# First phase of a fused MetaFormer kernel: projection and residual one slot later, values last in slot 1, tie break and block scaling in fewer instructions

## The reference

```
value, feat = conv1x1(x, v_w, v_b), conv1x1(x, f_w, f_b)      # heads of 24 channels, image in 2 x 2 quarters
centers, value_centers = pool(feat), pool(value)               # 2 x 2 centres of each quarter
sim = sigmoid(beta + alpha * einsum('bmc,bnc->bmn', l2norm(centers), l2norm(feat)))
idx = argmax(sim, axis=1)                                      # the first centre wins a tie
sim = sim * (arange(M)[None, :, None] == idx[:, None, :])
agg = (einsum('bmn,bnc->bmc', sim, value) + value_centers) / (sum(sim, -1) + 1)
out = conv1x1(einsum('bmc,bmn->bnc', agg, sim), proj_w, proj_b)
```

## Time and profile before

| | |
|---|---|
| median of 3 runs | 3696.35 us (3695.0 to 3697.74) |
| the profiled execution, its own time | 3702.22 us |
| its span in the trace | 3700.4 us |
| mean granted TensorE clock | 0.907 |
| DVE's last instruction of the first phase | about 2048 us from the start of the span |

### The profile page before, as it was taken

How to read it: one execution, slowest core, us unless ns; L and a number is a source line. 1 busy time by engine, 2 the same in 40 slices (tenths; PEclk the granted TensorE clock), 3 DMA queues, 4 the chain that set the end, 5 groups by cost and what they waited for, 6 DMA issues and landing times. The chain is left out here.

```text
span 3700.4 us, 65658 instructions
## 1 busy us (share of the span) xinstructions
PE 2912.9 (79%) x20710; PEld 1897.5 (51%) x20710; DVE 3193.9 (86%) x8131; ACT 2787.9 (75%) x6274; POOL 1729.4 (47%) x2404
## 2 busy tenths in 40 slices
PE   5777777777777776767776799998788888888887
PEld 5565656565655555656553344443444444444444
DVE  4888888888888888888887699999799999999998
ACT  2577777777777777777777555554699999999998
POOL 3777777777777777777765000000122222222221
PEclk8788888888888888888887799999899999999999
DMA  3232323232323232323211788898666677667762
GB/s 67 53 78 78 78 78 79 77 84 73 84 73 87 69 87 73 86 71 86 72 55 52 197 237 235 236 276 228 168 189 179 185 200 193 177 186 197 196 177 80
DMA packets 696169, 478.77 MB, mean 129 GB/s; under 512 B 407217, under 2 KB 674422, under 8 KB 683830
## 3 DMA queue, kind: packets, MB, share of 16 engines
q1 hardware_dynamic: 695830, 474.58, 48.6%
HBM read 272.09 MB, written 201.92 MB: 128 GB/s over the span
## 5 line engine op out<-in xcount | busy, mean ns | idle before, releaser
L1882 POOL TENSOR_SCALAR C_var<-C_st 128x16 f32<-128x16 f32 x64 | 13.6, 212 | 1342.3 <-DVE C_st L178 1342.3
L1455 DVE SCALAR_TENSOR_TENSOR B_y<-B_mid,B_coefs,B_y 128x512 f32<-128x512 f32 x768 | 509.0, 738 | 3.2 <-ACT B_y L1420 3.2
L1386 PE MATMUL B_ps_row<-B_z,B_band 128*128 128x512 f32 x1152 | 497.3, 594 | 14.9 <-DMA B_band<-edge_scratch 14.9
L378 DVE TENSOR_SCALAR A_hq<-A_h,A_b 128x512 f16<-128x512 f16 x768 | 296.4, 422 | 233.3 <-ACT A_h L370 226.9
L370 ACT ACTIVATE A_h<-A_hid 128x512 f16<-128x512 f32 x768 | 427.1, 591 | 64.8 <-PE A_hid L357 61.5
L178 DVE BATCH_NORM_STATS2 A_st<-A_xT 128x6 f32<-128x192 f32 x1536 | 443.9, 349 | 26.9 <-ACT A_xT L852 13.6
L370 ACT ACTIVATE C_h<-C_hid 128x512 f16<-128x512 f32 x768 | 425.4, 589 | 22.5 <-PE C_hid L357 22.3
L1495 ACT ACTIVATE C_q<-C_xT,C_shift,C_rstd 128x96 fp8e5<-128x96 f32 x1024 | 392.5, 457 | 46.4 <-POOL C_shift L1889 46.3
L167 POOL TENSOR_TENSOR A_rstd<-A_var,A_expo 128x16 f32<-128x16 f32 x128 | 374.4, 2925 | 10.7
L885 ACT ACTIVATE A_xc<-A_xT,A_shift,A_rstd 128x96 f32<-128x96 f32 x1024 | 379.1, 456 | 0.0
L1386 PEld LDWEIGHTS B_ps_row<-B_z,B_band 128*128 128x128 f32 x1152 | 218.1, 190 | 292.9 <-issue 285.1
(11 more groups left out here) (165 smaller groups left out, 6997.2 us busy)
## 6 DMA issues: line engine op xcount, KB each, us to landing
A_xq<-in_x SPq DMA_DIRECT2D x32, 1536.0 KB, 8.9
x_scratch<-A_xT SPq DMA_DIRECT2D x64, 768.0 KB, 3.2
x_scratch<-A_x3h SPq DMA_DIRECT2D x64, 768.0 KB, 5.4
B_z<-x_scratch SPq DMA_DIRECT2D x96, 512.0 KB
y_scratch<-B_y SPq DMA_DIRECT2D x96, 512.0 KB, 3.6
C_x3q<-x_scratch SPq DMA_DIRECT2D x32, 1536.0 KB, 9.2
C_xT<-x_scratch SPq DMA_DIRECT2D x64, 768.0 KB, 16.5
C_y3q<-y_scratch SPq DMA_DIRECT2D x31, 1536.0 KB, 15.7
```

The costliest lines, as they stand in the source:

```text
L378: r = dve.tensor_scalar(self.hq[:, b, s], self.h16[:, b, s], self.w["b1"][:, j:j + 1], 0.0, ALU.add, ALU.max)
L1386: m = pe.matmul(bank(c, h), band[c.buf(NB)][:, d, :], z[c.buf(NB)][:, half(h), d:d + W], start=(d == 0), stop=(d == 2))
L1455: dve.scalar_tensor_tensor(y, mid[c.buf(2)][:, half(h), t:t + W], coefs[:, c.n, 3 + t:4 + t], y, ALU.mult, ALU.add).then_inc(ev["sums"], 1)
```

## The change

- `project` (PE) and `projected` (DVE) are in slot 3 instead of 2; mixer output, residual and its statistics in slots 4 to 7 instead of 3 to 6; the turns of the similarity in slots 6 and 8 instead of 5 and 7.
- `values` is PE's last piece of slot 1; `sum_out` is DVE's first of slot 1, `own_heads` is in slot 2 behind `dve_hidden`, and so are the cosines in theirs. `similarity` comes ahead of the slot's statistics.
- The running maximum of the tie break is kept in spare elements of `eq` (nine per head instead of four), which saves its first copy; two instructions are left of three.
- `pabd` is written by one instruction over 128 partitions, with a table of own blocks from the constants (ones and zeros) as third operand.
- POOL's `pool_norm` of chunks 2 and 3 goes ahead of `ln2` of the second half.
- agg's bank is now given free by the second `gathered` event instead of the first. The two lists of ring uses follow the new order.

```diff
-OUT_AT = {3: (0, 1), 4: (2, 3), 5: (4, 5), 6: (6, 7)}
+OUT_AT = {4: (0, 1), 5: (2, 3), 6: (4, 5), 7: (6, 7)}
-SIMT_AT = {5: 0, 7: 1}
+SIMT_AT = {6: 0, 8: 1}
-AGG_AT, SUM_AT, VAL_AT, PA_AT = 8, 0, 1, 2
+AGG_AT, SUM_AT, VAL_AT, HEADS_AT, PA_AT = 8, 0, 1, 2, 3
...
-            if s == VAL_AT:
-                front_uses.append(("val", 0, 1, "aT4", 0))
             front_uses += [("big", c, 2, "big", c) for c in BIG_AT.get(s, ())]
...
             if s == SUM_AT:
                 front_uses.append(("sum", 0, 1, "summed", 0))
+            if s == VAL_AT:
+                front_uses.append(("val", 0, 1, "aT4", 0))
...
-                front_uses.append(("agg", 0, 2, "gathered", 0))
+                front_uses.append(("agg", 0, 2, "gathered", 1))
...
+        own_block = cst[:, K_BLOCK:K_BLOCK + TPC]
-        eq = sb("A_eq", [P, NT * HEADS, M], F32)
-        taken = sb("A_taken", [P, NT * HEADS, M - 1], F32)
+        eq = sb("A_eq", [P, NT * HEADS, M * (M - 2) + 1], F32)
...
@@ PE body @@
-                    if q1.real and s == VAL_AT:
-                        values(i)
                     if i.real and s + 1 < NK:
...
                     if q1.real and s == SUM_AT:
                         sum_rows(i)
+                    if q1.real and s == VAL_AT:
+                        values(i)
...
@@ similarity @@
-                dve.tensor_copy(taken[:, u, 0], e[:, :, 0]).then_inc(ev["tie"], 1)
                 for m in range(1, M - 1):
-                    dve.wait_ge(ev["tie"], ev.at("tie", q, (M - 1) * h + m - 1))
-                    dve.tensor_tensor(taken[:, u, m], taken[:, u, m - 1], e[:, :, m], ALU.max).then_inc(ev["tie"], 1)
-                dve.wait_ge(ev["tie"], ev.at("tie", q, (M - 1) * h + M - 2))
-                dve.tensor_tensor(e[:, :, 1:M], e[:, :, 1:M], taken[:, u, :], ALU.is_gt).then_inc(ev["only"], 1)
+                    if m > 1:
+                        dve.wait_ge(ev["tie"], ev.at("tie", q, (M - 2) * h + m - 2))
+                    dve.tensor_tensor(eq[:, u, M * m], eq[:, u, M * (m - 1)], e[:, :, m], ALU.max).then_inc(ev["tie"], 1)
+                dve.wait_ge(ev["tie"], ev.at("tie", q, (M - 2) * h + M - 3))
+                dve.tensor_tensor(e[:, :, 1:M], e[:, :, 1:M], eq[:, u, 0:M * (M - 2) + 1:M], ALU.is_gt).then_inc(ev["only"], 1)
...
@@ projected @@
-                for t in range(TPC):
-                    g = slice(32 * t, 32 * t + 32)
-                    m = dve.tensor_scalar(pabd[g, t * C:(t + 1) * C], s_pa[g, 0:C], rden[g, :], None, ALU.mult)
-                m.then_inc(ev["pabd"], 1)
+                dve.scalar_tensor_tensor(pabd[:].rearrange("p (t c) -> p t c", c=C),
+                                         s_pa[:, 0:C].unsqueeze(1).to_broadcast([P, TPC, C]), rden[:],
+                                         own_block.unsqueeze(2).to_broadcast([P, TPC, C]),
+                                         ALU.mult, ALU.mult).then_inc(ev["pabd"], 1)
...
@@ DVE body @@
-                    if q1.real and s == VAL_AT:
+                    if q1.real and s == SUM_AT + 1:
+                        sum_out(q1)
+                    if i.real and s < NK:
+                        ff.dve_hidden(dve, i, s)
+                    if q1.real and s == HEADS_AT:
                         own_heads(q1)
                     if q2.real and s in COS_AT:
                         cosines(q2, COS_AT[s])
-                    if i.real and s < NK:
-                        ff.dve_hidden(dve, i, s)
...
                     for k in OUT_AT.get(s, ()):
                         if q1.real:
                             x1(q1, k)
+                    if q2.real and s in SIM_AT:
+                        similarity(q2, SIM_AT[s])
...
-                    if q2.real and s in SIM_AT:
-                        similarity(q2, SIM_AT[s])
                     if q2.real and s == AGG_AT:
                         gather_out(q2)
-                    if q1.real and s == SUM_AT:
-                        sum_out(q1)
...
@@ POOL body @@
                 if q1.real:
+                    ff.pool_norm(pool, q1, 1)
                     ln2(q1, 1)
-                    ff.pool_norm(pool, q1, 1)
...
+    for t in range(TPC):
+        consts[32 * t:32 * t + 32, K_BLOCK + t] = 1
```

More of the change, by code:

```diff
@@ L53 @@
 K_QUARTERS = K_ROWS + HM
-K_W = K_QUARTERS + M
+K_BLOCK = K_QUARTERS + M
+K_W = K_BLOCK + TPC
 class Events:
@@ L471, in phase_a @@
                     c16=1, cw=1, cwc=1, big=NK, n2=NK, n2c=2, seed=2, rn_s=22, rn=2, guarded=2, cos=2, sig=2, mx=2, eq=2,
-                    tie=6, only=2, sim=2, simr=2, simT=2, side=1, sided=1, pool=1, agg=1, gathered=2, sum=1, summed=1, val=1,
+                    tie=2 * (M - 2), only=2, sim=2, simr=2, simT=2, side=1, sided=1, pool=1, agg=1, gathered=2, sum=1, summed=1, val=1,
                     rden=1, aT4=1, pa=1, pabd=1, bn3=NK,
@@ L1026, in similarity @@
                 s3 = sim[:, t, :].rearrange("p t (h m) -> p (t h) m", m=M)
-                e = eq[:, u, :]
+                e = eq[:, u, 0:M]
                 dve.wait_ge(ev["sig"], ev.at("sig", q, h))
@@ L1035, in similarity @@
                 dve.wait_ge(ev["eq"], ev.at("eq", q, h))
-                dve.tensor_copy(taken[:, u, 0], e[:, :, 0]).then_inc(ev["tie"], 1)
                 for m in range(1, M - 1):
-                    dve.wait_ge(ev["tie"], ev.at("tie", q, (M - 1) * h + m - 1))
-                    dve.tensor_tensor(taken[:, u, m], taken[:, u, m - 1], e[:, :, m], ALU.max).then_inc(ev["tie"], 1)
-                dve.wait_ge(ev["tie"], ev.at("tie", q, (M - 1) * h + M - 2))
-                dve.tensor_tensor(e[:, :, 1:M], e[:, :, 1:M], taken[:, u, :], ALU.is_gt).then_inc(ev["only"], 1)
+                    if m > 1:
[3 more added lines that the diff above has]
+                dve.tensor_tensor(e[:, :, 1:M], e[:, :, 1:M], eq[:, u, 0:M * (M - 2) + 1:M], ALU.is_gt).then_inc(ev["only"], 1)
                 dve.wait_ge(ev["only"], ev.at("only", q, h))
-                dve.tensor_tensor(sim32[:, t, 0:HM], sim[:, t, :], e.rearrange("p (t h) m -> p t (h m)", h=HEADS),
-                                  ALU.mult).then_inc(ev["sim"], 1)
+                dve.tensor_tensor(sim32[:, t, 0:HM].rearrange("p t (h m) -> p t h m", m=M),
+                                  sim[:, t, :].rearrange("p t (h m) -> p t h m", m=M),
+                                  e.rearrange("p (t h) m -> p t h m", h=HEADS), ALU.mult).then_inc(ev["sim"], 1)
             def gather_out(q):
```

## The result

The changed kernel takes 3822.27 us, the median of 4 runs (3820.12 to 3828.27); in the same comparison the kernel before took 3696.83 (3695.0 to 3697.74). The ratio is 1.0345, with a 95% interval of 1.0332 to 1.0358. The forecast was 3667, in a range of 3625 to 3725: wrong in sign and outside the range.

A forecast was written before the change was run, and what follows sets the result against it. No engine was full, DVE nearest at 86%, leading from T to H and ACT from H to T. Steps of 44.2 + 16.1 = 60.3 us against 61.3 save 29 us over 29 steps: 3667 us, range 3625 to 3725.

The forecast's parts named there:

- T to H: From ACT's third hidden copy's end in slot 0 (T) to DVE's slot 7 rounding's end (H): 49.6 to 44.2 us.
- no-change rival: POOL's loop, reckoned at 59.9 us, runs a little longer beside DVE and takes the rest: 3696 us, 12%.
- Slot 1, values last (−3.8): In slot 1, PE's 2.16 us values wait goes and DVE's rounding ends at T + 3.85, not T + 7.7: gain 3.8.
- The waits in slots 3 and 4: DVE waits for ACT, late through POOL's norm work: 0.9 us lost in slot 3, 0.7 more in slot 4.
- One block instruction (−0.7): Projection in slot 3: one 0.60 us DVE instruction replaces four taking 1.33 us, saving 0.7 a step.
- Tie break (−0.5): Two DVE copies of 0.25 us each go, saving 0.5 a step; stride of nine costs nothing, bounds −0.1 to +0.4.
- Residual a slot later (−2.0): Residual adds and statistics of chunks 6 and 7 leave the stretch before H, saving 2.0 us; covered by DVE waits after H.
- H to T (16.1): From DVE's slot 7 rounding's end to ACT's third hidden copy in the next slot 0: 11.7 grows to 16.1 us.
- the residual of chunk 6: After H, fwd chunk 4 waits for this add's bank until H + 2.0, delaying ACT's y copy to H + 3.7: +2.5 us.
- agg: After H, its 1.77 us of PE matmuls wait for fwd 5's bank; line 896 starts at H + 10.0: +1.0 us.
- clock rival: PE's clock stays down from agg through slot 1, 1.5 us a step worse than before: 3740 us, 17%.
- The sum: Steady step of 44.2 + 16.1 = 60.3 us against 61.3, 1.0 us saved in each of 29 full steps.

The follow-up runs named there:

- tiny passes: POOL's centring and scaling of the FFN input cut to one channel of 96, waits kept: 3677.9 us in the changed kernel, 3690.1 in the kernel before.
- kernel 5: Changed kernel with DVE's similarity put back behind the slot's statistics, as before the change: 3839.3 us, ratio 1.0391.
- (8): Kernel before with only the shorter tie break and the single block-scaling (pabd) instruction, no piece moved: 3697.9 us, ratio 1.0001.
- kernel 6: Changed kernel with POOL's centring and scaling of the FFN input on one channel of 96, waits and events kept: 3677.9 us, ratio 0.9955.
- kernel 7: Kernel before with POOL's centring and scaling of the FFN input on one channel of 96, waits and events kept: 3690.1 us, ratio 0.9987.
- kernel 15: Kernel before with values last, both instruction cuts, and POOL's pass of chunks 4 and 5 moved right behind chunks 2 and 3: 3642.5 us, ratio 0.9842.

## Why the prediction was wrong

**The step that failed** is the costing of the moved DVE work at the durations that it had in its old place, and with it the sentence that phases two and three are untouched and the two swapped POOL calls "only let the q8 of chunks 2 and 3 go ahead of a wait on chunk 7". The forecast followed POOL's passes as something that others wait for, never as something that runs beside DVE. With tiny passes T to H is 43.8 us, against a forecast of 44.2, and with the real ones 48.7. That term, put at nothing and measured at 4.9 us a step, is the miss; 144 us in all. The signs were in the trace of the kernel before, but not in the rows chosen: slot 3's three relus at 1.44 instead of 0.86 (line 378 at 1066.35, beside POOL's line 229), and the adds of 0.98 and 1.07 shown above. (The 0.90 for two relus in the earlier trace rows is no such sign: with tiny passes that pair still takes 0.84.) The no-change rival spoke of slower POOL passes beside DVE. That is a small part of it: POOL's pass takes 1.61 + 1.60 us beside the 3.64 us pair, but the scaling pair of the next pass takes 1.71 beside slot 7's relus, and 2.04 in kernel 5 beside the rounding and the adds. The engine that loses most is DVE.

The Trainium skill ("SBUF — State Buffer", section "SBUF: two separate sides") says that DVE and GpSimd share a pair of SBUF ports as an exclusive lock: a DVE instruction in a two-port mode, or one with two SBUF inputs against a GpSimd instruction that reads SBUF, and the GpSimd instruction block each other for the whole instruction of the one that started first. The traces agree on which forms meet: adds with one operand in PSUM (1.00 for two) and statistics (2.20 for eight) are not touched. On how long, they agree in part. Where POOL's pass had started first, DVE's instructions were held each for the rest of one POOL instruction, as in this step of the kernel after, in which the tie break's pair was through before the pass began (three rows of DVE's timeline, then one of POOL's):

```profile
1417.17 0.59 DVE L1042 TENSOR_TENSOR A_eq<-A_eq 128x64 f32<-128x64 f32 x2
1417.80 0.96 DVE L1044 TENSOR_TENSOR A_eq<-A_eq 128x192 f32<-128x192 f32 x1
1418.79 0.95 DVE L1046 TENSOR_TENSOR A_sim<-A_sim,A_eq 128x256 f32<-128x256 f32 x1
...
1417.65 1.80 POOL L221 TENSOR_TENSOR A_xc<-A_xT,A_st 128x384 f32<-128x384 f32 x2
```

They do not agree where DVE's instruction starts at the same moment as POOL's: the 64-element one, recorded as starting 8 ns ahead of the pass (1021.565 and 1021.573; POOL's recorded times are rough), took 3.3 us, over four POOL instructions of 0.8, where by the rule it would go first.

**Slot 1, values last (−3.8).** The waits went as forecast: line 730 starts without one, the granted clock is 1.00, the rounding ends at T + 4.5 (forecast T + 3.85). In the kernel before the term is covered by the pass of chunks 4 and 5 (5.6 us alone, none of it in the steady steps); with it out of the way the step is 59.6 us and not 61.4, 1.8 of the 3.8, with the two cuts in it. **The waits in slots 3 and 4** came as forecast: DVE waits 0.80 us for ACT in slot 3 (forecast 0.9) and 1.43 in slot 4 (forecast 1.5), in the mean of the steps.

**One block instruction (−0.7)** measured 618 ns, 0.60 forecast: right as to its length. **Tie break (−0.5)**: the stride costs nothing (276 ns). Yet the two cuts gain nothing alone (8): DVE waits for ACT instead. **Residual a slot later (−2.0)**: covered after H, as said, but with it went what DVE does beside POOL's passes, and that was not followed.

**H to T (16.1)** measured 17.2, and 17.7 with tiny passes. PE waits for the residual of chunk 6 at H + 2.0, exactly the step forecast, and ACT's y copy starts at H + 3.9 (forecast 3.7). What was mis-sized is agg and what follows it. The timelines of PE and of ACT after H = 1030.50:

```profile
1032.53 0.90 PE L676 MATMUL A_fbank<-A_cst,A_xq 96*128 96x96 f32 x4 [7.01 <-DVE A_xT L1083]
1038.29 2.79 PE L713 MATMUL A_fbank<-A_xT,A_simr 128*32 128x96 f32 x64 [1.10 <-ACT A_xT L853]
```

```profile
1034.42 0.49 ACT L328 ACTIVATE A_y<-A_bbank 128x384 f16<-128x384 f32 x1 [0.47 <-PE A_bbank L298]
...
1041.97 1.44 ACT L897 ACTIVATE A_x3h<-A_bbank,A_gb 96x512 f32<-96x512 f32 x2 [2.51 <-PE A_bbank L781]
```

Agg takes 2.79 us at a granted clock of 0.50, and not the 1.77 of the earlier trace rows; PE stood for 7.01 before the fwd turns and 1.10 before agg. Not every step is like this: over the steps between 900 and 1500 us agg takes 2.47 in the mean, and line 897 starts at H + 11.4 (10.1 to 11.9) and not H + 10.0. With tiny passes PE stands only 2.8 before the fwd turns and agg still takes 2.79 in each step, so the collisions are not what makes it slow. The clock rival was right about this stretch and wrong about slots 0 and 1, where the clock is full. H to T is 1.1 us a step of the 5.6 that the forecast missed.

**The sum.** Without the collisions the step is 61.4 us (17.7 + 43.8), that of the kernel before, and not 60.3; the 16 us that kernel 6 wins on the kernel before (12 on kernel 7) come from the fill and the last passes: from the first to the last start of its line 1164, the once-a-unit copy, it takes 1839.3 us against 1856.0, with equal steps between. The forecast had set these ends at nothing, within 6. So even without the collisions the steady step gains none of the 1.0 us forecast, and the whole is worth half of the 29. That T to H then comes out near its forecast is in part chance: DVE waits 2.8 us in slot 4 there, where 1.5 were forecast.

Three slips in the working decide nothing: the three costs from H to T add up to 4.2 and are used as 4.1, POOL's row ends at T + 7.0 by its own figures and not T + 7.3 (measured T + 6.8), and the 0.92 for two line 1079 instructions is not in the earlier trace rows, which has their mean of 546 ns.

**The rivals** missed the mechanism: none priced a DVE instruction that POOL holds up, and the one that ended slower gave 3740, 82 us below the measured time.

## What to carry to other kernels

When work of DVE is moved, or when POOL's is, lay the two timelines side by side at the new positions and mark which DVE instructions have two SBUF inputs or are relus and roundings on 16-bit data: beside POOL's passes each of them took here 0.5 to 0.6 us longer, less than one POOL instruction of 0.8, and 3 us longer where it started together with a pass of four. A collision showed up as a busy time far above the group's usual one and never as a wait, so look at the largest duration of a small instruction and not at its median. And a gain can be real and hidden by one pass that stood in a wait: kernel 15 gained 56.5 us by the removed wait and the cuts (4.7 alone) together with the moved pass (nothing alone).

## What the runs showed of the hardware

A DVE instruction of 276 ns was held for 3.32 to 3.33 us while POOL ran four instructions back to back, in 27 steps of the kernel after: it did not get its turn between two of them, and POOL's own kept their 0.80 us each. With tiny passes the same instruction in the same place takes 0.28. In kernel 5 the compare of 256 elements, which starts 0.11 us ahead of POOL's scaling pair, is held over both of that pair (1.99 us, 0.43 alone).

Where a POOL pass was already running, DVE's instructions took their turns with it: relus 0.91 us each (0.35 alone), roundings 1.07 (0.56), 16-bit adds 0.98 (0.35), 32-bit adds with two SBUF inputs 1.07 (0.56). POOL's were then slowed as well, 1.80 us for a pair beside the tie break's compares and not 1.62. Statistics and PSUM-source adds on DVE ran beside the same passes at their usual spacing of 0.28 and 0.50 us.
